# A state-space and mixture-of-experts layer on one core: second products moved into the shared PSUM banks, a fourth decay bank, new places for most stages

## What is computed

```
x = x + 0.5 * ffn(layernorm(x))
x = x + mamba(layernorm(x))
x = x + 0.5 * ffn(layernorm(x))       # the same weights

ffn(v):    e = argmax(softmax(v @ Wg + bg))                  # one of 8 experts for each token
           return gelu(v @ W1[e] + b1[e]) @ W2[e] + b2[e]
mamba(v):  xp, z = split(rmsnorm(v) @ in_proj.T)             # 256 channels each
           xp = silu(causal conv over 4 tokens(xp) + conv_b)
           dt_x, B, C = split(xp @ x_proj.T)                 # 128, 16, 16
           dt = softplus(dt_x @ dt_proj.T + dt_proj_b)
           h[t] = exp(dt[t] * A) * h[t-1] + dt[t] * xp[t] * B[t]   # 256 channels x 16 states
           y[t] = sum over states (h[t] * C[t]) + D * xp[t]
           return (y * silu(z)) @ out_proj.T + v
```

## Time and profile before

| | us |
|---|---|
| median of 3 runs | 1627.05 (1619.66 to 1628.12) |
| the profiled execution, its own time | 1629.39 |
| its span | 1627.6 |
| TensorE busy | 1255.5 (77%) |
| GpSimd busy | 1067.3 (66%) |
| VectorE busy | 1060.8 (65%) |
| ScalarE busy | 834.0 (51%) |

### The profile page before, as it was taken

The page is one execution under the profiler, slowest core; times in us unless marked ns, Lnnn a source line. Parts: engine busy times, 40 slices in busy tenths (PEclk is TensorE's granted clock), DMA queues, the critical chain, the costliest instruction groups (busy, mean ns, idle before and its releaser), DMA issues.

```text
span 1627.6 us, 16260 instructions
## 1 busy us (share of the span) xinstructions
PE 1255.5 (77%) x5188; PEld 616.0 (38%) x5188; DVE 1060.8 (65%) x1713; ACT 834.0 (51%) x1171; POOL 1067.3 (66%) x900
## 2 busy tenths in 40 slices
PE   3787867687887877788787877788787878778677
PEld 1433414133343434344344333344343434324244
DVE  2113869677676676777677676867677676979810
ACT  1244545464555556464556556464566557374422
POOL 1016778768667587868668577858668668888510
PEclk9866759689888889898889889898889889877676
DMA  3004141404032221304032221303122221322000
GB/s 77 1 8 181 45 144 44 146 9 168 22 110 84 99 97 62 122 21 156 32 112 84 99 85 52 144 22 133 55 101 89 93 91 57 140 94 95 1 7 13
DMA packets 60405, 130.02 MB, mean 80 GB/s; under 512 B 7744, under 2 KB 26864, under 8 KB 52128
## 3 DMA queue, kind: packets, MB, share of 16 engines
q1 hardware_dynamic: 60320, 128.98, 23.1%
HBM read 106.94 MB, written 22.02 MB: 79 GB/s over the span
## 4 chain that ended last, share of the span: by engine, by line
PE 35%; DVE 26%; ACT 21%; POOL 8%; issue 8%; SPq 1%; DVEq 0%; DMA 0%; ACTq 0%; POOLq 0%
PE PH L459 12%; DVE dA L756 10%; PE PY L477 8%; PE G L446 7%; ACT dA L631 6%; DVE hb L760 5%; DVE hb L754 4%; PE PH L458 4%; POOL hb L933 3%; ACT hs L598 3%; ACT L598 2%; ACT L613 2%; DVE xs L773 2%; PE Y L489 2%; POOL xr L916 2%
## 5 line engine op out<-in xcount | busy, mean ns | idle before, releaser
L933 POOL TENSOR_TENSOR hb<-dtx_rep,bs 128x1024 f32<-128x1024 f32 x256 | 598.5, 2358 | 0.0
L756 DVE TENSOR_TENSOR_SCAN dA<-dA,hb 128x512 f32<-128x512 f32 x352 | 430.4, 1223 | 106.0 <-ACT dA L631 100.8
L631 ACT ACTIVATE dA<-dt_rep,A 128x512 f32<-128x512 f32 x512 | 340.5, 687 | 239.0 <-DVE hb L760 225.5
L459 PE MATMUL PH<-xnT,W 128*128 128x512 f32 x512 | 352.5, 776 | 0.0
L477 PEld LDWEIGHTS PY<-W,hs 128*128 128x128 f32 x2048 | 298.6, 221 | 125.0 <-issue 113.5
L941 POOL TENSOR_TENSOR hb<-hb,cs 128x1024 f32<-128x1024 f32 x80 | 188.3, 2354 | 239.1 <-DVE hb L754 239.1
L477 PE MATMUL PY<-W,hs 128*128 128x128 f32 x2048 | 339.7, 316 | 0.0
L754 DVE TENSOR_TENSOR_SCAN hb<-dA,hb 128x512 f32<-128x512 f32 x160 | 186.4, 1206 | 183.4 <-ACT dA L631 175.8
L596 ACT COPY hs<-PH 128x512 f32<-128x512 f32 x160 | 93.5, 584 | 353.2 <-PE PH L459 353.0
L458 PE MATMUL PH<-ohT,Lm 24*128 24x512 bf16 x256 | 112.6, 440 | 201.4 <-ACT hs L598 172.1
L760 DVE TENSOR_TENSOR hb<-dA,cs 128x512 f32<-128x512 f32 x352 | 243.3, 691 | 25.2 <-DVE dA L756 0.9
(11 more groups left out here) (86 smaller groups left out, 1210.4 us busy)
## 6 DMA issues: line engine op xcount, KB each, us to landing
dtx_rep<-dtx_rows SPq DMA_DIRECT2D x32, 1024.0 KB, 6.7
dt_rep<-dt_rows SPq DMA_DIRECT2D x32, 1024.0 KB, 7.9
bs<-bc_rows SPq DMA_DIRECT2D x64, 256.0 KB, 3.7
cs<-bc_rows SPq DMA_DIRECT2D x64, 256.0 KB, 3.7
dtx_rows<-dtx SPq DMA_DIRECT2D x32, 256.0 KB, 2.5
dt_rows<-dt SPq DMA_DIRECT2D x32, 256.0 KB, 2.6
X<-in_x SPq DMA_DIRECT2D x16, 256.0 KB, 3.0
out<-X SPq DMA_DIRECT2D x16, 256.0 KB, 2.4
```

The source lines that it names most:

```text
L459: nc.tensor.matmul(PH[:, :], W1[:, e, :], xnT[:, w, :], start=False, stop=True).then_inc(ph_full, 1)
L631: nc.scalar.activation(dA[u % NA][:, :], dt_rep[:, h, g, :], ACT.Exp, scale=A[:, h, g, q:q + 1]).then_inc(decay, 1)
L756: nc.vector.tensor_tensor_scan(a, a, x_in_hb, 0.0, ALU.mult, ALU.add).then_inc(scan, 1)
L933: nc.gpsimd.tensor_tensor(hb[:, s % HR], dtx_rep[:, h, 2 * m:2 * m + 2, :], bs[:, q, None, :].broadcast_to([P, 2, CH]), ALU.mult).then_inc ...
```

## The change

- The bank PY is given up. The second products of f1 and f2 become two more stages, `py_f1` in G0 and `py_f2` in G1, which hold their bank from the first expert's matmul until VectorE has added it to x. `g_full` of that bank is raised by TensorE's sequencer after the last expert, so that the counts of the bank stay right; VectorE itself still waits for `w2_done`.
- The eighth bank becomes a fourth decay bank (`NA = 4`), so that the exponential of unit u waits for unit u-4.
- The second products move: those of f1 to slots 1, 2 and 3, those of f2 to slots 12, 13 and 14. Before, f1's were in slots 4 to 9, f2's in slots 12 to 15, 0 and 1.
- On ScalarE the silu block moves from slot 3.0 to 5.5, the gelu block of f2 from 7.5 to 9.5, taps from 14.5 to 11.0; the gelu block of f1 stays at 15.5. Softplus (dt1, dt0, exp, ln) moves from 6.0 to 7.0 to 8.0 to 9.0.
- Almost all other stages get new slots. The convolution for chunk i0+2 now comes before TensorE's last read of x of chunk i0, so `xs` gets a third buffer (`RX`). x is loaded five chunks ahead, not four. Nothing is computed differently and the number of instructions of each kind stays.

```diff
-NA = 3
+NA = 4
+RX = 3
...
-STAGES = [("ln_f1", 3, 0, 1, 0), ("z0", 1, 1, 1, 2), ("z1", 1, 0, 2, 2), ("gate_f1", 3, 0, 3, 2),
...
+STAGES = [("py_f1", 2, 0, 1, 1.5), ("ln_f1", 3, 1, 1, 2), ("gate_f1", 3, 1, 2, 2), ("z0", 1, 1, 4, 1), ("z1", 1, 0, 5, 0),
+          ("out", -1, 0, 6, 1), ("ln_p", 2, 0, 7, 0), ("bc", 1, 1, 7, 1), ("dt1", 1, 0, 7, 2), ("dt0", 1, 1, 8, 0),
+          ("oh_f1", 3, 0, 8, 2), ("x1", 2, 0, 9, 2), ("x0", 2, 1, 9, 2), ("py_f2", -2, 1, 12, 1.5), ("ln_f2", -1, 0, 12, 2),
+          ("gate_f2", -1, 0, 13, 2), ("oh_f2", -1, 0, 15, 0)]
...
+ACT_AT = {"ln_f1": 2.0, "silu": 5.5, "ln_p": 7.5, "bc": 8.0, "dt1": 8.0, "dt0": 8.5, "exp": 9.0, "ln": 9.0, "gelu_f2": 9.5,
+          "taps": 11.0, "ln_f2": 13.0, "gelu_f1": 15.5}
+DVE_AT = {"y_f2": 0.5, "stats_f1": 1.0, "gated1": 2.0, "gate_f1": 3.5, "y_f1": 4.0, "stats_p": 4.5, "out": 6.5, "stats_f2": 6.5,
+          "oh_f1": 9.5, "gated0": 10.0, "tap01": 11.5, "tap2": 12.0, "gate_f2": 14.5, "oh_f2": 15.5}
+POOL_AT = {"root_p": 5.0, "norm_p": 6.0, "root_f2": 8.0, "dt": 9.5, "dtx": 10.0, "norm_f2": 11.0, "root_f1": 13.0,
+           "norm_f1": 14.0}
...
-W2_AT = [[(s, 2) for s in (4, 5, 6, 7, 8, 8, 9, 9)],
-         [(12, -2), (12, -2), (13, -2), (14, -2), (15, -2), (0, -3), (0, -3), (1, -3)]]
+W1_AT = [[(11, 0, 3), (12, 0, 3), (13, 0, 3), (14, 0, 3), (15, 0, 3), (15, 1, 3), (0, 0, 2), (0, 0, 2)],
+         [(2, 0, -2), (3, 0, -2), (6, 0, -2), (7, 0, -2), (8, 0, -2), (9, 1, -2), (10, 0, -2), (10, 0, -2)]]
+W2_AT = [[(s, 2) for s in (1, 1, 1, 2, 2, 2, 3, 3)], [(s, -2) for s in (12, 12, 12, 13, 13, 13, 14, 14)]]
...
-        PY = psum("PY", [P, CH])
...
             def second_product(it, w, e, off):
...
+                b = G_AT[f"py_f{w + 1}"][0]
+                PY = G[b]
                 if e == 0:
...
+                    it.wait_free(pe, g_free, f"py_f{w + 1}")
...
                 last.then_inc(w2_done[w], 1)
+                if e == E - 1:
+                    pe.sem_inc(g_full[b], 1)
...
                 if t == DVE_AT["y_f2"] and it.has(-3):
                     it.wait(dve, w2_done[1], -3, E, E)
-                    add_to_x(X[:, it.tiles(-3), :], PY, 0.5, y_added[1])
+                    b = G_AT["py_f2"][0]
+                    add_to_x(X[:, it.tiles(-3), :], G[b], 0.5, g_free[b])
```

More of the change, by code:

```diff
@@ L54 @@
 G_AT = {name: (bank, off) for name, bank, off in G_SEQ}
[L56 to L62, removed]
+ACT_AT = {"ln_f1": 2.0, "silu": 5.5, "ln_p": 7.5, "bc": 8.0, "dt1": 8.0, "dt0": 8.5, "exp": 9.0, "ln": 9.0, "gelu_f2": 9.5,
[4 more added lines that the diff above has]
+           "norm_f1": 14.0}
+SP_AT = {"x_out": 1, "x_in": 4, "bc": 9, "b0": 10, "dt": 10, "b1": 10, "c0": 10, "b2": 12, "c1": 12, "b3": 14, "dtx1": 14,
          "c2": 14, "dt1": 15, "c3": 15}
-W1_AT = [[(9, 0, 3), (10, 0, 3), (11, 0, 3), (13, 0, 3), (14, 0, 3), (15, 0, 3), (0, 0, 2), (0, 1, 2)],
-         [(1, 0, -2), (2, 0, -2), (3, 0, -2), (5, 0, -2), (6, 0, -2), (7, 0, -2), (8, 0, -2), (8, 1, -2)]]
-W2_AT = [[(s, 2) for s in (4, 5, 6, 7, 8, 8, 9, 9)],
-         [(12, -2), (12, -2), (13, -2), (14, -2), (15, -2), (0, -3), (0, -3), (1, -3)]]
+W1_AT = [[(11, 0, 3), (12, 0, 3), (13, 0, 3), (14, 0, 3), (15, 0, 3), (15, 1, 3), (0, 0, 2), (0, 0, 2)],
+         [(2, 0, -2), (3, 0, -2), (6, 0, -2), (7, 0, -2), (8, 0, -2), (9, 1, -2), (10, 0, -2), (10, 0, -2)]]
+W2_AT = [[(s, 2) for s in (1, 1, 1, 2, 2, 2, 3, 3)], [(s, -2) for s in (12, 12, 12, 13, 13, 13, 14, 14)]]
 W1_ORDER = sorted((s, k, w, e, off) for w in range(2) for e, (s, k, off) in enumerate(W1_AT[w]))
@@ L348, in store_x @@
                 dst, src = od[:, J * (it.i0 - 3):J * (it.i0 - 2), :], X[:, it.tiles(-3), :]
-                it.wait(sp_, y_added[1], -3, 1, 1)
+                it.before().wait_read(sp_, g_free, "py_f2")
                 sp_.dma_start(dst, src).then_inc(x_out, 16)
@@ L401, in body @@
                         store_x(it)
-                    if s == SP_AT["x_in"] and it.has(4) and it.i0 + 4 > 0:
+                    if s == SP_AT["x_in"] and it.has(5) and it.i0 + 5 > 0:
                         load_x(it)
@@ L641, in stages @@
                 if t == ACT_AT["taps"] and it.has(2):
-                    it.wait(act, summed, 0, 8, 5)
+                    it.wait(act, summed, 2 - RX, 8, 8)
                     for h in (1, 0):
@@ L733, in norm_stats @@
             def norm_stats(it, w, off):
+                it.wait(dve, moments[w], off, 1, 0)
                 for j in range(J):
@@ L772, in convolve @@
                     src = G[b][:, :].rearrange("p (b l) -> p b l", b=NB)
[L773 to L774 removed]
+                    last = nc.vector.scalar_tensor_tensor(xs[:, (it.i0 + 2) % RX, h, :, sh:L], src[:, :, 0:L - sh], Wc[:, h, k:k + 1],
+                                                          xs[:, (it.i0 + 2) % RX, h, :, sh:L], ALU.mult, ALU.add).then_inc(conv, 1)
                     if k == K - 2:
@@ L850, in stages @@
                 if t == DVE_AT["stats_p"] and it.has(2):
-                    it.wait(dve, y_added[0], 2, 1, 1)
+                    it.wait_read(dve, g_free, "py_f1")
                     norm_stats(it, 2, 2)
```

29 lines of the change are left out of this document (11 added, 18 removed), and 3 rows, old and new, of the table STAGES.

## The result

The change makes the kernel slower: 1674.66 us (median of 4 runs, 1667.95 to 1685.61) against 1625.82 us, a ratio of 1.031 with a 95% interval of 1.025 to 1.038. The forecast was 1630 us; the result lies at the upper end of the range, beside the second rival (1676 us). The medians of e2 and e8 in the table further down include one slow execution each (1659.6 and 4592.8 us); the ratios leave these out.

The account below looks back on a forecast made before the run. It took a ring as the bound: TensorE's late first products hold ScalarE, whose queued decays starve VectorE. From the profiled 1629.4 us, + 11 x 0.75 - 12 + 5 gave 1630.6, forecast 1630 us, range 1578 to 1676.

Parts of the forecast that it names:

- Rival 2: Low clock catches both gelu blocks (9.9 us each) and the second-product stretch: 97.3 us a period, 1676 us; chance 0.20.
- The walk through the order: VectorE's waits added up slot by slot over one period at full clock: 20.8 us of waits, period 89.3 us.
- one unit (1.9 us) off behind each gelu block: After gelu blocks: the fourth bank lets ScalarE be four units ahead, covering one more unit, 1.9 us.
- The step that failed: Clock cost per period: 1.2 us f2 gelu block, 2.2 second-product stretch, 0.5 ln_p; 3.9 in all, making 93.2.
- 12 us of gain: Four lighter iterations at the scan's start and end: fourth bank brings some 3 us each, bounds 0 and 6.
- 5 were taken: Before the scan: chunk 1's second products stand ahead of chunk 0's B, C and dt, costing 0 to 9 us.
- the sum: Whole kernel: profiled time 1629.4 + 11 x 0.75 - 12 + 5 = 1630.6 us.
- some 8 us after these blocks: After gelu blocks: fourth bank and freed blocks remove some 8 us of waits; the stretches give most back.
- called excluded: Fourth bank doing nothing was ruled out, since decays wait for unit u-4 in the list.
- The prediction's price for giving up PY: f2's second products wait for the shared bank: period 93.2 us, against 90.7 with an own bank, 2.5 us.
- Rival 1: TensorE's clock stays up on the path: period 89.3 us, 1588 us in all; chance 0.20.
- Rival 3: Gain not given back: TensorE-stretch waits and half the clock's cost vanish, about 86 us a period, 1551 us; chance 0.08.

Follow-up runs that it names:

- e2: Changed kernel with three decay banks and the eighth bank given to both second products: 1637.0 us, 1.008 of the kernel before.
- e8: e1 plus matmuls of no use beside the gelu blocks only (ahead of experts 6 and 7), written to the unused bank: 1591.9 us, 0.980 of the kernel before.
- e11: Changed kernel (four decay banks) plus matmuls of no use beside gelu blocks, in banks in use, none in the last two f2 blocks: 1608.1 us.
- e15: e11 with three decay banks, nothing else changed: 1616.4 us, 0.994 of the kernel before.
- e13: e2 plus matmuls of no use beside the gelu blocks only, none in the last two f2 blocks: 1572.4 us, 0.967 of the kernel before.
- e1: Changed kernel with three decay banks again and the eighth bank left unused: 1685.5 us, 1.037 of the kernel before.
- e9: e1 plus matmuls of no use only before out, ln_p and f2's second products: 1689.4 us, 1.038 of the kernel before.
- e3: e1 plus matmuls of no use in seven places, beside the gelu blocks and before out, ln_p and f2's second products: 1608.2 us.

## Why the prediction was wrong

**The walk through the order held in size.** It named the large waits of VectorE, and the period that it gave for full clock was 89.3 us. e11, the changed kernel with the clock up beside the gelu blocks, has nine periods from 513.10 to 1331.31 us (the starts of the first table load of silu's block), 90.9 us each, at a clock of 0.90. The stretch of second products is still at the lower clock there; with the prediction's own 2.2 for it and 0.5 at ln_p the walk gives 92.0, 1.1 too much. One part of it did not hold: it took one unit (1.9 us) off behind each gelu block for the fourth bank, and e15, with three banks, has full periods as short as e11's. Something else in the walk must then have been counted too dear; what, stays open. (Its 24.3 us of waits before the change are ten waits, not nine.)

**The step that failed is the clock's.** "I take half of that difference for the f2 block (1.2), 2.2 for the stretch and 0.5 at ln_p", 3.9 us in all, nothing for the block of f1. In the trace after, the f2 block took the whole difference (9.9 us against 7.6, 2.3), the f1 block 9.4 us (1.8), the stretch 2.3. That is 3.0 us a period more than the three terms had, and the period became 96.0, 6.7 above the full-clock walk and 2.8 above the forecast's 93.2. e11 confirms it: with both blocks at 7.6 us the same kernel takes 67 us less. The prediction had the rows to see it: the earlier trace rows showed a block with nothing between its products at 9.9 us, and the change makes both blocks such blocks. In the kernel before, second products stood between the first products of experts 6 and 7, and after them the W1 part of expert 7's was back at 1.12 us (the row at 831.37 above), where after the change it takes 2.08. I read them as delay, took them out of the path, and counted the relief at full clock.

**The lighter iterations and the ends.** Cut both profiles at the first scan by line 754 of each iteration. The eleven full periods then cost 41.4 us more than before (the forecast had 8), and the four lighter intervals 4.1 us more (315.4 against 311.3), where 12 us of gain were forecast. The first of these scans is 9.2 us later (169.85 against 160.7 us) and the first scan of all 5.9 (158.61 against 152.69), where 5 were taken. From the last of these scans to the end the changed kernel is 7.2 us shorter, where nothing was taken. Together that is the 46 us between the sum (1630.6) and the profiled execution's own time (1676.74): 33 + 16 + 4 - 7. The 12 us of the lighter iterations failed by the clock as well, since in e11 they take 302.3 us, 9 less than before.

**The fourth bank.** It was counted as covering one unit more behind each block, "some 8 us after these blocks" together with the freed blocks, and that it does nothing was called excluded. Alone it is worth 11 us in the whole kernel at the lower clock and 8 at the higher, and in the full periods nothing (96.0 us with it and 95.4 without; 91.0 and 90.7 with the added matmuls). The 3 us that the prediction gave it in each lighter iteration are near what it does there at the higher clock (13 us in four).

**The shared bank.** The prediction's price for giving up PY was 2.5 us a period, 28 in all. With the gelu blocks at full clock it measured 2.25 a period (e13 against e8), so the price was right; at the low clock it became 3.9 a period and 48.5 us in the whole kernel (e1 against e2). The Trainium skill, Perfetto Trace Analysis, section Optimizing Tensor Performance (Matmuls), asks for rotation of independent groups of matmuls through different banks; both numbers agree with its direction.

**Rival 2** had the mechanism and nearly the size: "both blocks then take 9.9 us as in rows 8, the stretch runs at the lower clock": 97.3 us a period and 1676 us, against 96.0 and 1674.7. It should have been the forecast, with the same rows. It isn't right in its parts: the f1 block took 9.4 us, and the ends cost 6 us and did not save 7, which the shorter period makes up for. Rival 1 supposed the higher clock everywhere; e11 has it beside the gelu blocks alone and lands at 1608 us, 20 above rival 1's 1588. Rival 3 did not occur.

## What to carry to other kernels

When a change takes work out of a hand-off between TensorE and another engine, price what is left at the clock of a sparse TensorE, as some row of the trace shows it, and not at the clock that it had with that work in between. Where a round trip over one bank is on the path and TensorE has nothing to do meanwhile, try to put independent work there (its own, if the list has any; matmuls of no use otherwise), and only there: the same matmuls elsewhere raised the clock and gained nothing (e9), and on top of those beside the gelu blocks they cost 16 us (e3 against e8). A further buffer for an engine that mostly waits for a third one buys little; here it helped the iterations with less work on TensorE and not the full ones.
